# A Perceiver layer on one core: identity products at both ends, a new order of the key splits, loads on a second queue, semaphore steps dropped

## The reference

```python
x = x + cross_attention(layernorm(x), ctx_768, ...)   # 16 heads of 64; 257 context rows of 192 channels
x = x + self_attention(layernorm(x), ...)             # 16 heads of 16 over the 32 tokens
x = x + channel_mix(layernorm(x), ...)                # token shift, sigmoid gate * (relu(k)^2 @ W_v)
```

## Time and profile before

| | |
|---|---|
| runs | 887.66, 888.2, 890.65 us, median 888.2 us |
| profiled execution | 890.68 us, of which the span from first to last instruction is 888.6 us |
| mean granted TensorE clock | 0.972 of full |
| PE busy | 811.1 us (91%) |
| DVE busy | 612.1 us (69%) |
| ACT busy | 598.0 us (67%) |
| POOL busy | 414.6 us (47%) |

### The profile page before, as it was taken

One profiled execution on the slowest core, in us unless ns is written; L12 is line 12 of the kernel. 1 busy time (PEld: TensorE's weight loads), 2 busy tenths in 40 slices (PEclk: granted clock), 3 DMA queues, 4 the chain that ended last, 5 costly groups with the idle time before them and its releaser, 6 DMA issues.

```text
span 888.6 us, 20369 instructions
## 1 busy us (share of the span) xinstructions
PE 811.1 (91%) x7279; PEld 662.5 (75%) x7279; DVE 612.1 (69%) x1857; ACT 598.0 (67%) x1423; POOL 414.6 (47%) x664
## 2 busy tenths in 40 slices
...
GB/s 216 120 13 37 25 61 13 26 26 25 49 16 34 25 60 14 25 25 39 35 25 25 25 61 13 26 25 67 8 25 25 37 37 12 13 26 16 11 1 13
DMA packets 49523, 30.51 MB, mean 34 GB/s; under 512 B 22928, under 2 KB 48336, under 8 KB 49424
## 3 DMA queue, kind: packets, MB, share of 16 engines
...
## 4 chain that ended last, share of the span: by engine, by line
PE 72%; DVE 13%; ACT 6%; issue 5%; SPq 1%; DMA 1%; POOL 1%; POOLq 0%; DVEq 0%; ACTq 0%
PE score L786 15%; PE post L872 5%; PE pre L671 5%; PE probT L797 5%; DVE qk_t L1270 4%; PE aux L730 3%; PE post L881 3%; PE ac_main L812 2%; PE ac_main L817 2%; PE ac_tail L818 2%; PE ac_tail L814 2%; PE ac_main L813 2%; DVE qk_l L1265 2%; PE post L852 2%; PE post L858 2%
## 5 line engine op out<-in xcount | busy, mean ns | idle before, releaser
L428 POOL TENSOR_TENSOR prT_l<-prT,prT_h 128x512 fp32r<-128x512 f32 x128 | 170.9, 1339 | 137.6 <-ACT prT_h L1066 137.0
L571 POOL TENSOR_SCALAR pr<-pr,rsum,poison 128x257 f32<-128x257 f32 x256 | 145.4, 578 | 187.1 <-DVE rsum L1295 186.7
L1289 DVE CUSTOM_DVE_ANT_0 sm<-score,mbias 128x257 f32<-128x257 f32 x256 | 108.1, 424 | 97.5 <-PE score L786 82.0
L1047 ACT ACTIVATE pr<-sm,nmx 128x257 f32<-128x257 f32 x256 | 129.2, 506 | 44.9 <-DVE nmx L1289 43.4
L786 PE MATMUL score<-cT_h,qk_h 128*128 128x258 f32 x256 | 92.5, 361 | 15.7 <-DVE qk_t L1270 11.4
L1055 ACT ACTIVATE prT<-probT 128x512 f32<-128x512 f32 x128 | 75.8, 592 | 23.7 <-PE probT L797 22.5
L1066 ACT ACTIVATE prT_h<-prT 128x512 fp32r<-128x512 f32 x128 | 79.5, 628 | 11.5 <-PE ac_tail L818 10.8
L797 PE MATMUL probT<-ident,pr 128*128 128x128 f32 x512 | 78.4, 276 | 4.3 <-POOL pr L571 3.9
L786 PE MATMUL score<-cT_h,qk_t 128*128 128x258 f32 x256 | 73.1, 286 | 0.0
L786 PE MATMUL score<-cT_l,qk_h 128*128 128x258 f32 x256 | 72.9, 285 | 0.0
L786 PE MATMUL score<-cT_h,qk_l 128*128 128x258 f32 x256 | 72.8, 284 | 0.0
...
## 6 DMA issues: line engine op xcount, KB each, us to landing
...
```

The costliest lines, as they stand in the source:

```text
L428: eng.tensor_tensor(prT_l[:, :, cut], prT[:, :, cut], prT_h[:, :, cut], ALU.subtract).then_inc(prob_lower, 1)
L571: last = pool.tensor_scalar(p, p, rsum[:, j % 2, t:t + 1], poison[:, 0:1], ALU.mult, ALU.mult)
L1047: act.activation(pr[j % 2][:, t, :], sm[:, t % 2, :], ACT.Exp, bias=nmx[:, j % 2, t:t + 1], scale=-1.0, accum_out=ssum[:, j % 2, t:t + 1]) ...
L1289: dve.tensor_tensor_reduce(sm[:, t % 2, :], score[t % 2][:, 0:NK], mbias[:], DH ** -0.5, BIG, ALU.add, ALU.min, nmx[:, j % 2, t:t + 1]).th ...
```

## The change

- PE's SETUP becomes `WARM XT WK0 WK1 LEFT WK2 WK3 Q0 Q1 CT0`. WARM is 18 products of the identity with itself into score bank 0, as soon as the identity exists. LEFT now goes to bank `ac_tail` and has semaphores of its own; it waits for the first two WK copies. H0 waits for two WK copies (`N_SETUP_KEYS`), the later H jobs for four.
- 21 jobs Z0 to Z20 are added to the closing's PE order, between its last jobs. Each is one product of the identity with 256 columns of `wo`, into bank `aux`, which is taken out of the closing's other uses. Nothing reads the result and nothing waits for it.
- All orders are rewritten. In the first group PE now does `H0 CT:1 G2 H2 G3 H4 H6 H8 S0:0 H10`, where it did `H0 G2 H2 S0:0 H4 H6 CT:1 G3 H8 H10`; ACT and DVE follow. POOL's LX moves forward to just after N0:0 in the middle groups, and XB ahead of CT:1.
- Eight loads (gamma, beta, last rows twice, mask four times) are issued by ACT at its start, ahead of its first work, and no longer by SP.
- `alone` and its uses are dropped.

```diff
 PE_FIRST = (
-    "H0 G2 H2 S0:0 H4 H6 CT:1 G3 H8 H10 S1:0 S2:0 LV0 S3:0 CT:2 S0:1 P0:0 S1:1 LV1 P1:0 S2:1 S3:1 CT:3 F0 S0:2 S1:2 S2:2 "
+    "H0 CT:1 G2 H2 G3 H4 H6 H8 S0:0 H10 S1:0 S2:0 CT:2 S3:0 S0:1 LV0 P0:0 S1:1 S2:1 P1:0 LV1 CT:3 S3:1 S0:2 S1:2 P0:1 "
+    "AC:0 S2:2 P1:1 S3:2 F0 S0:3 S1:3 S2:3 P0:2 CT:4 AC:1 XT F1 S3:3 P1:2 S0:4 S1:4 CT:5 AC:2 S2:4 Q0 P0:3 S3:4 P1:3 S0:5 "
...
 PE_LAST = (
-    "S2:7 S3:7 P1:6 AC:5 FR FK P0:7 AC:6 FV OT0.0 P1:7 OT1.0 WO.0 LT.1 AC:7 OT0.1 T2.0 OT1.1 QT.0 KT.0 WO.1 SC.0 VR.0 "
-    "T2.1 QT.1 KT.1 SC.1 VR.1 PT.0 PV.0 T4.0 PJ.0 PT.1 PV.1 T4.1 PJ.1 T3.0 T3.1 FR.0 FK.0 FR.1 FV.0 FK.1 FV.1").split()
+    "P0:6 FR FK S3:7 P1:6 FV P0:7 OT0.0 AC:6 P1:7 OT1.0 LT.1 WO.0 AC:7 OT0.1 T2.0 OT1.1 QT.0 KT.0 WO.1 Z0 Z1 SC.0 Z2 VR.0 "
+    "T2.1 Z3 QT.1 KT.1 Z4 Z5 Z6 Z7 Z8 Z9 Z10 SC.1 VR.1 PT.0 PV.0 Z11 T4.0 PJ.0 PT.1 Z12 PV.1 Z13 T4.1 Z14 PJ.1 Z15 Z16 "
+    "T3.0 Z17 Z18 Z19 Z20 T3.1 FR.0 FK.0 FR.1 FK.1 FV.0 FV.1").split()
 ACT_FIRST = (
-    "H0 H1 H2 G2 H3 CT:1 H4 H5 H6 G3 H7 H8 H9 H10 H11 CU:0 S0:0 S1:0 S2:0 S3:0 LV0 CT:2 CU:1 S0:1 P0:0 U0:0 S1:1 LV1 CT:3 "
+    "H0 H1 G2 H2 H3 H4 H5 G3 H6 H7 H8 CT:1 H9 H10 S0:0 H11 S1:0 CT:2 S2:0 S3:0 LV0 CU:0 P0:0 S0:1 S1:1 U0:0 P1:0 LV1 S2:1 "
...
 DVE_FIRST = (
-    "H0 H1 H2 H3 CT:1 H4 S0:0 H5 H6 H7 H8 H9 H10 H11 A0 A1 S1:0 R0:0 S2:0 S3:0 A2 A3 A4 A5 R1:0 A6 S0:1 CT:2 S1:1 S2:1 "
+    "H0 H1 H2 H3 H4 H5 H6 S0:0 H7 H8 H9 H10 H11 S1:0 CT:1 R0:0 S2:0 S3:0 R1:0 S0:1 CL:0 S1:1 A0 CT:2 S2:1 R0:1 A1 S3:1 A2 "
...
 DVE_LAST = (
-    "C2.0 C3.0 C4.0 C5.0 PJ.1 C6.0 C0.1 C7.0 C8.0 C1.1 C9.0 C2.1 C10.0 C3.1 C11.0 C4.1 C5.1 C6.1 C7.1 C8.1 C9.1 C10.1 "
-    "C11.1 M1.0 FR.0 M1.1 SG.0 FR.1 FV.0 SG.1 FV.1").split()
+    "C1.0 C2.0 C3.0 C4.0 C5.0 C6.0 C7.0 C8.0 C9.0 PJ.1 C0.1 C1.1 C10.0 C2.1 C11.0 C3.1 C4.1 C5.1 C6.1 C7.1 C8.1 C9.1 "
+    "C10.1 C11.1 M1.0 M1.1 FR.0 FR.1 SG.0 FV.0 SG.1 FV.1").split()
 POOL_ORDER = (
-    "CT:1 XB N0:0 CT:2 N1:0 L0:0 L1:0 N0:1 N1:1 CT:3 X1 N0:2 L0:1 L1:1 N1:2 CT:4 N0:3 L0:2 L1:2 N1:3 W0 W1 L0:3 N0:4 CT:5 "
+    "XB CT:1 N0:0 LX N1:0 CT:2 L0:0 L1:0 N0:1 CT:3 N1:1 L0:1 N0:2 N1:2 L1:1 X1 N0:3 CT:4 L0:2 L1:2 L0:3 W0 N1:3 W1 CT:5 "
...
-SETUP = "WK0 WK1 XT WK2 WK3 Q0 LEFT Q1 CT0".split()
+SETUP = "WARM XT WK0 WK1 LEFT WK2 WK3 Q0 Q1 CT0".split()
+N_WARM = 18
+N_SETUP_KEYS = (2, 4, 4, 4, 4, 4)
...
+            def keep_clock():
+                pe.matmul(aux[:, 0:256], ident[:], wo[:, 0, :], start=True, stop=True)
...
+                elif name == "WARM":
+                    for _ in range(N_WARM):
+                        pe.matmul(warm_bank[:, 0:P], ident[:], ident[:], start=True, stop=True)
...
                 dve.wait_ge(scores_done, n + 1)
                 after(dve, exp_done, n - 1)
-                alone(dve)
                 dve.tensor_tensor_reduce(sm[:, t % 2, :], score[t % 2][:, 0:NK], mbias[:], DH ** -0.5, BIG,
```

More of the change, by code:

```diff
@@ L64 @@
 PE_FIRST = (
[3 rows of a table removed]
-    "AC:5 P1:6 K4 K6 P0:7 LT AC:6 CT:0 P1:7 K8 K10 AC:7").split()
[3 rows of a table added]
+    "K2 AC:5 K4 P1:6 K6 P0:7 AC:6 K8 LT P1:7 CT:0 K10 AC:7").split()
 PE_ORDER = (
[3 rows of a table removed]
-    "S1:7 FR S2:7 P0:6 FK AC:5 S3:7 P1:6 FV K0 K2 AC:6 P0:7 LT K4 P1:7 K6 CT:0 K8 AC:7 K10").split()
[3 rows of a table added]
+    "S1:7 FR S2:7 P0:6 FK AC:5 S3:7 P1:6 FV K0 K2 AC:6 P0:7 LT K4 K6 P1:7 CT:0 K8 AC:7 K10").split()
 PE_LAST = (
[4 rows of a table removed]
-    "T2.1 QT.1 KT.1 SC.1 VR.1 PT.0 PV.0 T4.0 PJ.0 PT.1 PV.1 T4.1 PJ.1 T3.0 T3.1 FR.0 FK.0 FR.1 FV.0 FK.1 FV.1").split()
@@ L80 @@
-ACT_FIRST = (
[4 rows of a table removed]
-    "K3 P1:6 U0:6 AC:5 U1:6 K4 K5 K6 CU:7 P0:7 K7 AC:6 CT:0 U0:7 P1:7 K8 U1:7 K9 K10 K11 AC:7").split()
-ACT_ORDER = (
[4 rows of a table removed]
-    "P1:6 U0:6 U1:6 S3:7 K0 K1 K2 K3 AC:6 P0:7 U0:7 K4 K5 P1:7 K6 K7 U1:7 CT:0 K8 K9 K10 K11 AC:7").split()
-ACT_LAST = (
[5 rows of a table removed]
[5 rows of a table added]
+    "T3.0 Z17 Z18 Z19 Z20 T3.1 FR.0 FK.0 FR.1 FK.1 FV.0 FV.1").split()
+ACT_FIRST = (
[4 rows of a table added]
+    "AC:5 P0:6 CU:7 K4 U0:6 P1:6 U1:6 K5 K6 K7 AC:6 P0:7 K8 U0:7 P1:7 U1:7 K9 K10 K11 CT:0 AC:7").split()
+ACT_ORDER = (
[4 rows of a table added]
+    "U0:6 S3:7 U1:6 K0 LV1 K1 K2 K3 AC:6 P0:7 K4 K5 U0:7 P1:7 K6 K7 U1:7 CT:0 K8 K9 AC:7 K10 K11").split()
@@ L120 @@
+DVE_LAST = (
[7 rows of a table added]
+    "C10.1 C11.1 M1.0 M1.1 FR.0 FR.1 SG.0 FV.0 SG.1 FV.1").split()
 POOL_FIRST = (
-    "CT:1 N0:0 CT:2 N1:0 L0:0 N0:1 N1:1 L1:0 CT:3 N0:2 N1:2 CT:4 L0:1 L1:1 N0:3 L0:2 L1:2 N1:3 N0:4 CT:5 L0:3 N1:4 L1:3 "
-    "CT:6 N0:5 CT:7 L0:4 L1:4 N1:5 N0:6 L0:5 LX N1:6 L1:5 N0:7 N1:7 L0:6 L1:6 L0:7 L1:7 CT:0").split()
+    "CT:1 N0:0 N1:0 L0:0 CT:2 N0:1 L1:0 CT:3 N1:1 N0:2 L0:1 L1:1 CT:4 N1:2 LX CT:5 L0:2 L1:2 N0:3 N1:3 L0:3 N0:4 CT:6 "
+    "L1:3 N1:4 CT:7 N0:5 L0:4 N1:5 L1:4 N0:6 L0:5 L1:5 N1:6 N0:7 L0:6 L1:6 N1:7 L0:7 L1:7 CT:0").split()
@@ L123 @@
 POOL_ORDER = (
-    "CT:1 XB N0:0 CT:2 N1:0 L0:0 L1:0 N0:1 N1:1 CT:3 X1 N0:2 L0:1 L1:1 N1:2 CT:4 N0:3 L0:2 L1:2 N1:3 W0 W1 L0:3 N0:4 CT:5 "
-    "L1:3 N1:4 CT:6 L0:4 N0:5 CT:7 L1:4 N1:5 N0:6 L0:5 LX L1:5 N1:6 KA L0:6 L1:6 N0:7 N1:7 YO CT:0 L0:7 L1:7").split()
+    "XB CT:1 N0:0 LX N1:0 CT:2 L0:0 L1:0 N0:1 CT:3 N1:1 L0:1 N0:2 N1:2 L1:1 X1 N0:3 CT:4 L0:2 L1:2 L0:3 W0 N1:3 W1 CT:5 "
+    "N0:4 L1:3 N1:4 CT:6 L0:4 N0:5 CT:7 L1:4 N1:5 N0:6 L0:5 CT:0 L1:5 N1:6 KA L0:6 L1:6 N0:7 N1:7 L0:7 YO L1:7").split()
@@ L126 @@
 POOL_LAST = (
-    "CT:1 N0:0 XB CT:2 N1:0 N0:1 L0:0 L1:0 N1:1 CT:3 L0:1 N0:2 X1 N1:2 L1:1 CT:4 L0:2 W0 N0:3 N1:3 L1:2 W1 N0:4 L0:3 CT:5 "
-    "L1:3 N1:4 CT:6 N0:5 CT:7 L0:4 N1:5 L1:4 N0:6 LX L0:5 N1:6 L1:5 N0:7 L0:6 L1:6 KA N1:7 YO L0:7 L1:7 XB.0 X1.0 W.0 "
-    "X1.1 W.1 KA.0 CT:0 KA.1 YO.0 YO.1").split()
-SETUP = "WK0 WK1 XT WK2 WK3 Q0 LEFT Q1 CT0".split()
+    "N0:0 XB CT:1 N1:0 L0:0 CT:2 CT:3 L1:0 N0:1 N1:1 N0:2 L0:1 L1:1 CT:4 X1 N1:2 N0:3 L0:2 N1:3 L1:2 CT:5 W0 W1 N0:4 L0:3 "
+    "CT:6 N1:4 L1:3 CT:7 L0:4 N0:5 L1:4 N1:5 L0:5 N0:6 L1:5 N1:6 LX N0:7 KA L0:6 L1:6 N1:7 YO L0:7 XB.0 CT:0 L1:7 X1.0 "
@@ L133 @@
+    "X1.1 W.0 W.1 KA.0 KA.1 YO.0 YO.1").split()
+SETUP = "WARM XT WK0 WK1 LEFT WK2 WK3 Q0 Q1 CT0".split()
+N_WARM = 18
+N_SETUP_KEYS = (2, 4, 4, 4, 4, 4)
 QK_NEEDS = ("Q0", "Q1", "Q1", "Q2", "Q3", "Q3")
@@ L142 @@
 OF_GROUP = ("LX", "LT")
+FILL = tuple(f"Z{n}" for n in range(21))
 TP = TOK // 2
@@ L282, in perceiver_layer @@
         CLOSING_OT_BANKS = {"OT0.0": (post, pre), "OT1.0": (post, pre), "OT0.1": (score[0], score[1]), "OT1.1": (probT, ac_tail)}
-        CLOSING_BANKS = [(pre, post), (ac_main, aux, score[0], score[1], probT, ac_tail)]
-        wk_bank, left_bank = [ac_main, ac_tail, aux, post], score[0]
+        CLOSING_BANKS = [(pre, post), (ac_main, score[0], score[1], probT, ac_tail)]
+        wk_bank, left_bank = [ac_main, ac_tail, aux, post], ac_tail
+        warm_bank = score[0]
         SETUP_PRE_BANKS = {"XT": pre, "Q0": probT, "Q1": ac_main, "Q2": ac_tail, "Q3": pre}
@@ L326, in after @@
             eng.wait_ge(s, value)
-        def alone(eng):
-            eng.sem_inc(waits_passed)
         def nth(jobs, name, g):
@@ L456, in _ @@
             sp.dma_start(xn[:], token_rows(x_rows, 0)).then_inc(x_in, 16)
-            for n, v in ((G1, g1), (B1, be1)):
-                sp.dma_start(cols[:, n, :], column(v)).then_inc(ln1_in, 16)
             sp.dma_start(wk_main, Wkv[0:P, 0:NH * DH]).then_inc(wk_staged, 16)
@@ L462, in _ @@
             sp.dma_start(wq[:, :, 0:512], wq_columns[:, :, 0:512]).then_inc(wq_in, 16)
-            sp.dma_start(left_in[:, 0:DC], ctx_in[:, NKF, :]).then_inc(left_staged, 16)
-            sp.dma_start(left_in[:, DC:256], ctx_in[:, NKF, P:DC]).then_inc(left_staged, 16)
             load_ctx(0, 0)
-            for r in range(4):
-                sp.dma_start(mraw[r * NQ:(r + 1) * NQ, :], mask[0, 0, :, :]).then_inc(mask_in, 16)
             sp.dma_start(wq[:, :, 512:1024], wq_columns[:, :, 512:1024]).then_inc(wq_rest_in, 16)
@@ L549, in columns @@
                 after(pool, scores_done, (b - 1) * NT)
-                alone(pool)
                 r = int(name[2]) % 2
@@ L629, in run @@
                         job(name, g)
-            pool.wait_ge(setup_copied, N_SETUP)
+            pool.wait_ge(left_split, 1)
             pool.wait_ge(consts_made, 8)
```

41 lines of the change are left out of this document (27 added, 14 removed), and 65 rows, old and new, of tables (ACT_FIRST, ACT_LAST, ACT_ORDER, DVE_FIRST).

## The result

The changed kernel takes 897.5 us (median of four runs, 896.16 to 898.18) against 888.7 us before in the same comparison: a ratio of 1.0094, interval 1.0072 to 1.0117. It is slower by 0.9%. The forecast was 867.3 us, with the range 860 to 880.

What follows compares the result with a forecast made beforehand. PE was taken to bound the middle groups, with gains only at the two ends. Savings 0.8 + 9.3 + 1.0 + 1.5 + 8.3 = 20.9 us from 888.2 gave 867.3 us, range 860 to 880.

Steps and rivals of the forecast that it cites:

- Middle groups: Six middle groups: new orders win 0.1 to 0.2 us a group, 0.7 in all; with `alone` dropped, 1.0 us saved.
- The slower rival: Middle groups: POOL's earlier XB and LX cost PE over 3.5 us a group; at 4.5, 894 us; chance 0.10.
- The setup: Kernel's start: earlier key-weight loads let H0 start at 21.0 instead of 21.82 us, 0.8 us saved; Q0 stays slow.
- The key stage: First group's key products and splits: S1:1 comes 20.3 us after H0 instead of 29.6; 9.3 us saved, and lasting.
- The last group: Last group before its closing: neighbouring jobs mostly swapped by one place; bounds -4 and +4 us, taken 1.5 us saved.
- The closing: Kernel's end: Z products in PE's waits keep the clock up, slow jobs shrink by 45%, 8.3 us saved.
- `alone`: Masks: dropping it removes an instruction between wait and operation; bounds 0 and 3 us, taken 0.3 saved.

## Why the prediction was wrong

**The step that failed is "Middle groups"**: "New orders can win at most some 2 us a group and I take 0.1 to 0.2". Reasoning from PE's idle 2.4 us in 100 bounds what orders can gain, and I let it stand for what they can cost. A loss has no such bound: a job that comes later on another engine holds a bank, and PE with it. What had to be done for each order was to ask, for every copy out of a bank, what stands ahead of it, when that now runs and who asks for the bank next: FV behind CL:7, K2 asking 0.9 us after PE's FV ends, 0.15 us to spare before the change, and CL:7 now beside POOL's subtractions. The runs gave it a price: 2.85 us a group of FV's place, of which 1.8 wait and 1.0 clock, and 1.4 us a group of the other moves, together 25.6 us.

**The slower rival** had the right size, 4.5 us a group and 894 us, and the wrong place. It looked only at POOL's XB and LX, and neither held PE in the changed kernel. The run with POOL's new order alone lost more than the rival asked for, 5.8 us a group, but at N1:3 behind L0:3. That 894 came near 897.5 is luck. Its chance of 0.10, and all bounds of the middle, were too small for a change that rewrites four orders.

**The setup** was given 0.8 us; H0 came 2.7 earlier. WARM brought the WK transposes to the full rate (in the timelines the pairs stand 0.46 us apart, before 0.71); I had them slow as before. XT didn't fit into the wait as counted: it began at 8.18 us and the first WK at 8.68. But Q0 was slow, 3.52 us, as forecast. The reason isn't settled: behind WARM all eight pairs of WK transposes ran at the full rate, the four behind the 0.81 us of standstill too, and the granted clock fell only from 13 us on (0.61 from 13 to 14, 0.50 from 14 to 16). With four products in the 0.81 us ahead of LEFT, Q0 takes 1.99. The rule quoted from the Trainium skill (TensorE: Matmul & The Clock Gate, "Part 4: PE-mode transpose"), that transposes don't count as work for the clock, does not hold in the closing, where 84 of them held it at 1.00; the measurement decides. What stays open is why 6.4 us of transposes and nothing else didn't bring PE to the full rate in the kernel before. The clock column is no help there: from 9 to 20 us of the kernel before it reads 1.00, while Q0 takes 3.60 us, so at the start of an execution the rate is read from the durations.

**The key stage** was right in its mechanism up to the last split and too large in size: S0:0 stood 11.5 us after H0 (counted 10.7 to 11.4) and the last split ended 17.6 us after it (16.5). But S0:1 came at 20.6 (18.0) and S1:1 at 23.9 (20.3), behind waits of 0.86 and 1.39 us for DVE and products at half clock from 38.5 us on. So the step gave 5.7 us, not 9.3; S1:1 at 43.07, 8.4 us earlier (forecast 41.4 and 10.1), owes the rest to the setup's 2.7. CT:4 came 7.9 us earlier. "From then on the first group has the same jobs left" was the wrong step: the jobs are the same, their order isn't, and it took 4.5 us more to OT0. The run with the old first group says that nothing of the 9.3 us arrives.

**The last group** gained 5.0 us up to WO.1 (6.8 to OT0.0, of which 2.3 are AC:6 gone behind that mark), not 1.5: the one place where PE was idle 10.7 us in 80 had some 1 us more to give than the bound of 4 that I had set. No run takes its orders apart.

**The closing** was right in its mechanism: clock 1.00, SC.1 1.07 us as written. That 8.2 us met 8.3 is partly luck: what the clock gives back is 7.0 us in the profiled executions and 4.4 by the medians, and the rest comes from the job order, which had been given less than 0.5. A Z was mis-sized: two records of 0.23 us, so 0.46 (a row counts records, two for a float32 product, and I had read them as products; Q0's "eight products" are four); the 21 take 9.6 us and are hidden all the same. WARM's 18 took 6.59 us, not 4.0, for the same reason, though a good third of its 36 records, the last ones, ran at the full rate.

**`alone`** was right: 888.4 against 888.0 us.
